# Adding four weighted corners of a sample: one strided VectorE reduction in place of two additions, in a deformable convolution on one Trainium2 core

## The reference

```
x = x + halo_attention(gn(x))     # 8x8 blocks, 14x14 windows, 4 heads
x = x + lstm(gn(x)) @ W_lin.T     # rows as sequences of 96 steps, hidden 128
x = x + deform_conv(gn(x))        # this is where the change lies
x = x + M @ blocks(gn(x)) @ M.T   # 8x8 blocks
```

```
x_off = g_lt * gather(qx_lt, qy_lt) + g_rb * gather(qx_rb, qy_rb)
      + g_lb * gather(qx_lt, qy_rb) + g_rt * gather(qx_rb, qy_lt)
x_off = x_off * mask              # (b, c, h, w, 9)
out   = conv3x3_stride3(x_off)
```

## Time and profile before

| | |
|---|---|
| median of three runs | 4143.36 us (4128.45 to 4147.88) |
| the profiled execution | 4145 us |
| its span | 4143.0 us, mean TensorE clock 0.67 |
| TensorE busy | 2422.6 us (58%) |
| VectorE busy | 2127.4 us (51%), 4233 instructions |
| ScalarE busy | 1085.4 us (26%) |
| GpSimd busy | 2652.4 us (64%), 2614 instructions |
| chain of work that ended last | GpSimd's gathers L563 47%, issue 14% |

### The profile page before, as it was taken

One profiled execution on the slowest core, in us unless ns is written; L12 is line 12 of the kernel. 1 busy time (PEld: TensorE's weight loads), 2 busy tenths in 40 slices (PEclk: granted clock), 3 DMA queues, 4 the chain that ended last, 5 costly groups with the idle time before them and its releaser, 6 DMA issues.

```text
span 4143.0 us, 53002 instructions
## 1 busy us (share of the span) xinstructions
PE 2422.6 (58%) x19232; PEld 1995.3 (48%) x19232; DVE 2127.4 (51%) x4233; ACT 1085.4 (26%) x2749; POOL 2652.4 (64%) x2614
## 2 busy tenths in 40 slices
PE   4877776787777658857776478657775211111112
PEld 3656664565666646636665356446664211111112
DVE  4753225787444568855445678644447323222222
ACT  2643332443322324423223144322221100000000
POOL 1000004777777767777777777777777777777775
PEclk9976667777566677866667678756667555555555
DMA  5531003663311246633113266431113212111111
GB/s 178 176 87 31 1 1 125 185 182 102 87 50 50 89 137 181 171 80 87 51 50 104 76 191 180 108 93 50 50 49 112 73 53 62 52 51 51 52 52 49
DMA packets 192844, 373.96 MB, mean 90 GB/s; under 512 B 59312, under 2 KB 89264, under 8 KB 192576
## 3 DMA queue, kind: packets, MB, share of 16 engines
q1 hardware_dynamic: 107256, 198.54, 15.8%
q0 software_dynamic: 82944, 170.04, 15.4%
q10 hardware_dynamic: 2384, 2.00, 0.2%
HBM read 265.15 MB, written 104.33 MB: 89 GB/s over the span
## 4 chain that ended last, share of the span: by engine, by line
POOL 47%; issue 14%; PE 1%; DVE 0%; ACT 0%; POOLq 0%; DMA 0%; DVEq 0%; ACTq 0%
POOL got L563 47%; PE bank L1290 0%; PE bank L1234 0%; PE gates L1500 0%; PE bank L1295 0%; PE gates L1491 0%; PE bank L1275 0%; POOLq L560 0%; ACT kp L627 0%; DVE k L899 0%; DVE k L905 0%; DVE got L844 0%; DMA got<-sample_table,index 0%; ACT q L608 0%; DVE red L846 0%
## 5 line engine op out<-in xcount | busy, mean ns | idle before, releaser
L563 POOL DMA_INDIRECT got<-sample_table,index x2592 | 2639.0, 1018 | 1435.1 <-issue 774.4
L1416 PE MATMUL gates<-hist,whh 128*128 128x96 f32 x3040 | 638.8, 379 | 303.5 <-DVE hist L1094 302.5
L1234 PE MATMUL bank<-turned,wout 128*128 128x96 f32 x1728 | 325.2, 369 | 748.3 <-DVE x L859 507.0
L1416 PEld LDWEIGHTS gates<-hist,whh 128*128 128x128 f32 x3040 | 576.6, 283 | 374.2 <-DVE hist L1094 372.8
L844 DVE TENSOR_TENSOR got<-got,weight 128x1152 f32<-128x1152 f32 x288 | 391.0, 1358 | 689.6 <-DMA got<-sample_table,index 689.1
L1234 PEld LDWEIGHTS bank<-turned,wout 128*128 128x128 f32 x1728 | 313.6, 281 | 764.4 <-DVE turned L853 758.7
L1087 DVE TENSOR_TENSOR prod<-sig,gc 128x192 f32<-128x192 f32 x384 | 133.9, 349 | 633.3 <-ACT sig L714 633.3
L925 DVE TENSOR_REDUCE mx<-gates 128x2 f32<-128x392 f32 x576 | 295.7, 553 | 137.2 <-PE gates L1313 127.3
L1406 PE MATMUL gates<-xs,wa 128*128 128x192 bf16 x768 | 256.0, 333 | 102.5 <-ACT sig L718 65.4
L646 ACT ACTIVATE pt<-gates 98x512 f32<-98x512 f32 x384 | 217.7, 593 | 287.7 <-PE gates L1327 283.3
L1408 PE MATMUL gates<-ones,bw 96*128 96x192 bf16 x768 | 261.8, 341 | 0.0
(11 more groups left out here) (134 smaller groups left out, 3505.9 us busy)
## 6 DMA issues: line engine op xcount, KB each, us to landing
kst<-k_parts SPq DMA_DIRECT2D x96, 441.0 KB
got<-sample_table,index POOLq DMA_INDIRECT x2592
qst<-q_parts SPq DMA_DIRECT2D x96, 288.0 KB
k_parts<-kp SPq DMA_DIRECT2D x24, 882.0 KB
k_parts<-kp SPq DMA_DIRECT2D x24, 588.0 KB
q_parts<-qp SPq DMA_DIRECT2D x24, 576.0 KB
sample_table<-tab SPq DMA_DIRECT2D x8, 1568.0 KB
q_parts<-qp SPq DMA_DIRECT2D x24, 384.0 KB
```

Of the source, the lines that this page charges most:

```text
L563: pool.indirect_dma_start(out=got[:, uu % RING, n, :], out_offset=None, in_=tables[p], in_offset=bass.IndirectOffsetOnAxis(ap=at, axis=0)) ...
L1234: mm = pe.matmul(out_ps[n % 2][:, at:at + GN], wout[:, tap, :], turned[:, k % 2, tap, :], start=(tap == 0), stop=(tap == NTAP - 1))
L1416: mm = pe.matmul(gate[n][:, h:h + W], whh[:, HID * g:HID * (g + 1)], hist[:, (t - 1) % HIST, :], start=False, stop=True, skip_group_check= ...
```

## The change

The tile `red` and the semaphore `summed` are gone. In `unit`, behind the multiplication, one `tensor_reduce` over the innermost axis reads `got` of the slot seen as (tap, channel, corner), so that the four corners of a channel, 32 numbers (128 bytes) apart, follow one another, and writes `samp` directly. It carries the signal `reduced`, on which GpSimd's ring slot and the transpose now both wait. The wait for `samp_turned` stands in front of it.

```diff
--- before.py
+++ after.py
@@ -210,7 +210,6 @@
         index = sb("index", [P, SLOTS2, CH, NTAP], I32)
         weight = sb("weight", [P, SLOTS2, CH, NTAP, 4])
         got = sb("got", [P, RING, NTAP, 4 * C])
-        red = sb("red", [P, NTAP, 2 * C])
         samp = sb("samp", [P, NTAP, C])
         turned = sb("turned", [P, 2, NTAP, GN])
 
@@ -380,7 +379,6 @@
         gathered = [sem(f"gathered{i}") for i in range(RING)]
         weighted = sem("weighted")
         reduced = sem("reduced")
-        summed = sem("summed")
         samp_turned = sem("samp_turned")
         convolved = sem("convolved")
         rows_added = sem("rows_added")
@@ -843,11 +841,9 @@
                 w = weight[:, chunk, uu % CH].rearrange("p n k -> p (n k)").unsqueeze(2).to_broadcast([P, NTAP * 4, C])
                 dve.tensor_tensor(corners, corners, w, ALU.mult).then_inc(weighted, 1)
                 dve.wait_ge(weighted, uu + 1)
-                dve.tensor_tensor(red[:, :, :], got[:, slot, :, 0:2 * C], got[:, slot, :, 2 * C:4 * C], ALU.add).then_inc(reduced, 1)
+                wait(dve, samp_turned, uu)
+                dve.tensor_reduce(samp[:, :, :], got[:, slot].rearrange("p n (k c) -> p n c k", c=C), AX.X, ALU.add).then_inc(reduced, 1)
                 dve.wait_ge(reduced, uu + 1)
-                wait(dve, samp_turned, uu)
-                dve.tensor_tensor(samp[:, :, :], red[:, :, 0:C], red[:, :, C:2 * C], ALU.add).then_inc(summed, 1)
-                dve.wait_ge(summed, uu + 1)
                 if i == 0:
                     wait(dve, convolved, k - 1)
                 dve.transpose(turned[:, k % 2, :, BLK * i:BLK * (i + 1)], samp[:, :, :]).then_inc(samp_turned, 1)
```

## The result

The change costs 2.95%: 4263.32 us in the median of six runs (4252.51 to 4278.82) against 4144.09 us of six runs of the kernel before (4128.45 to 4149.98), a ratio of 1.0295 with a 95% interval from 1.0269 to 1.0321. The forecast was 4262 us. The profiled execution took 4262.68 us, with a span of 4260.9 us.

What follows compares the result with a forecast made beforehand. VectorE's main stream was taken to bound until 1552 us, gathers from there to the end. 65.7 + 1.7 + 30.8 + 21.8 + 1.2 - 2.3 = +118.9 us on 4143.4 gave 4262 us, range 4136 to 4318.

Steps and rivals of the forecast that it cites:

- The reduction is slow because each number lies far from the last, not because of its kind: In each unit's reduction on VectorE: reads 128 bytes apart slow it from 1.36 us to 2.45 us; chance 0.66.
- free-stride rival: The reduction's stride costs nothing: 1.30 to 1.36 us, at most 0.1 us extra per unit, 4143 us; chance 0.24.
- Its size, 2.45 us: The strided reduction's duration, by L1050's factor of 1.9 on 1.04 ns per element; 1.19 us more per unit.
- lower bound of 4218 us: Low end of the forecast's own range: reduction 2.27 us, attention's share 0.71, 1.01 us extra per unit.
- LSTM of image 1, all 31 units in full: In image 1's LSTM each unit is the late side, so all 31 units count in full; 401 to about 438 us.
- Attention of image 1, 0.85 of each unit: In image 1's attention, 28 units count at 0.85, above the mean unhidden share of 0.71: 23.8 units.
- The first gather of image 2's round: At 1552 us: 65.7 us later from VectorE's main stream, plus 1.7 us for the slot's later release.
- Images 2 and 3: what the waits cover: Of 72.6 and 73.8 us added, data waits cover 41.8 and 52.0 us, leaving +30.8 and +21.8 us.
- The last stretch, nearly nothing: Behind 3222 us units lie under waits: +1.2 us for the last unit, -2.3 us for shorter gathers.
- The reduction does not hold GpSimd: Gathers starting during the one-input reduction are not held, as in L951: 0.94 us.
- Both rivals with a hold: Reduction holds GpSimd's gathers: fast, about 1.3 us, 4160 us, chance 0.04; or slow, 4475 us, chance 0.06.
- Signs: Expected profile: VectorE's gather waits 689 to about 600 us, GpSimd's slot waits 100 us or more, gathers' mean within 20 ns.

Runs made afterwards that it cites:

- dense kernel of part 1: The changed kernel with its reduction reading four neighbouring numbers (another sum): 4147.23 us, ratio 1.0002 to the kernel before; ratio 1.0015 on the 5355 us chip.
- VectorE's extra 0.79 us per unit: The kernel before plus one dense 576-number reduction per unit, result unread, behind the slot's release: 0.9975 on the 5355 us chip, 1.0199 (4233.63 us) on the 4154 us chip.

## Why the prediction was right

Its steps, one by one:

- *The reduction is slow because each number lies far from the last, not because of its kind.* Shown: dense 1353 ns, strided 2121 ns, and with the dense one the loss is gone (1.0002). The free-stride rival's own figure, 4143 us, is what the dense run gave (4147).
- *Its size, 2.45 us.* Too dear: 2.12 us. The factor of 1.9 came from L1050, which is of the fast kind with two reads at a time; a reduction loses 0.67 ns on 1.04 ns, a factor of 1.6. The other row, L1176 with 0.82 ns more per element, led to 2.27 us and was nearer (its own figures, 0.16 + 1152 x 1.86 ns, give 2.30 us, which moves the lower bound of 4218 us up by some 5 us). The text itself had named what spoke against L1050. Per unit that is 0.86 us in place of 1.19 us.
- *LSTM of image 1, all 31 units in full.* The mechanism is right: its steps with a unit went from 4.49 to 5.37 us, those without from 3.81 to 3.83 us. The stage grew by 28.9 us, 0.93 us per unit; to 431 us, not to 438, which is the size of the unit.
- *Attention of image 1, 0.85 of each unit.* Too kind. The stage grew by 26.0 us, and since the 4.3 us of data waits in it went to nothing, VectorE's own stream grew by 30.3 us: 1.08 us for each of 28 units, more than the 0.86 us that was put in. VectorE's waits for TensorE's scores grew in it from 30.0 to 38.4 us, and the granted TensorE clock fell from 0.73 to 0.70, so part of it may be matmuls that ran slower; that share was not measured by itself. The mean share of 0.71 was too low to begin with: image 0's window started at 20 us, but VectorE writes the first strip of its attention at 32.15 us, and that of image 1 at 696.48 us. From these to 290 and 1028 us it is 257.9 and 331.5 us, so 73.6 of 87 us were not hidden, 0.85.
- *The first gather of image 2's round.* Forecast 65.7 + 1.7 = 67.4 us later, measured 64.9 us. The dear unit and the kind share cancelled in the sum. The further 1.7 us for the slot cannot be told apart; moving the release alone behind the second addition cost nothing (1.0013).
- *Images 2 and 3: what the waits cover.* This is the step that was furthest off. It took the 41.8 and 52.0 us of waiting off in full. With the measured 0.86 us and 72 units that would leave 62 - 42 = 20 us for the second round and 10 us for the third; measured were 48.5 and 28.4 us. The waits for gathers did go to nothing, but other waits came. VectorE's waits for TensorE's scores in the attention of image 2, before and after (1504:1855 and 1564:1938 us), show it:

```profile
DVE mx L925 <- PE gates L1313: 27.8, 20, 4.0
```

```profile
DVE mx L921 <- PE gates L1309: 40.5, 21, 4.4
```

  In image 3's attention they went from 30.1 to 40.6 us. In the LSTM of the second round some 11 us more are in steps that hold no unit (their mean went from 3.68 to 3.86 us while the granted clock fell from 0.66 to 0.60), in that of the third 5 us (0.63 to 0.60). In the other runs on the chips of 4144 and 4154 us the clock of these LSTM stages lay between 0.58 and 0.68, so part of this loss may belong to the run and not to the change. Why the new waits came is argued, not tested: while VectorE waits for data, TensorE and ScalarE get ahead, and a wait that is filled takes that lead away too.
- *The last stretch, nearly nothing.* It gained 18.6 us where -1.1 us was forecast. GpSimd's group in this stretch, before and after (3234:4143 and 3370.6:4261 us), accounts for it:

```profile
L563 POOL DMA_INDIRECT got<-sample_table,index x689 | 668.1, 970 | 210.0 <-issue 210.0
```

```profile
L561 POOL DMA_INDIRECT got<-sample_table,index x680 | 652.7, 960 | 207.2 <-issue 207.2
```

  Busy and issue time are 878.1 us before and 859.9 us after, 18.2 us less. Nine gathers fewer are left, since GpSimd enters the stretch one unit further ahead (with 1912 gathers done in place of 1903, at 210 units on VectorE in both: 2.4 in place of 1.4 units): 9 x 1.27 = 11.5 us. The others are 10 ns shorter, 680 x 0.010 = 6.8 us: fewer holds, of which the forecast credited 2.3 us. The prediction left the longer lead out.
- *The reduction does not hold GpSimd.* Shown by 257 gathers at 0.94 or 0.95 us. Both rivals with a hold are out. (In the fast one the gather at 2602.48 us starts 0.3 us behind L849's start and not before its end; its price stays the same.) The Trainium skill (SBUF — State Buffer, Who interferes with whom), which the prediction left open, says so of `tensor_reduce` on trn2, and the trace agrees.
- *Signs.* VectorE's wait was to fall to about 600 us and fell to 507; GpSimd's slot waits were to be over 100 us and are 218.5; the gathers' mean was to stay within 20 ns and went from 1018 to 1003.

The sum, 118.9 us against 117.9 us by the spans, is closer than its terms deserve, and that is luck: a unit priced 0.33 us too dear and 17.5 us that the last stretch gave beyond the forecast were made up for by shares and covers that were too kind. Right were the cause, the side that is late in each stretch, and roughly where the loss falls.

## What to carry to other kernels

Fewer instructions are no gain where the one that stays reads one float of every 16 bytes: here 1.35 us became 2.12 us, more than the 1.22 us of the two dense additions that it replaced. If four summands must be innermost, let the producer (here, the table in DRAM) lay them side by side, or keep the dense additions. And when work is added to an engine that is not the bottleneck of the whole run, price it by stretch, and do not take waits off in full: of the 94 us in hand, about half was cover (2 x 62 us were added, 77 us were lost), though not a microsecond of these waits was left.

## What the runs showed of the hardware that was not expected

- **Two kinds of chip.** On two chips the kernel before takes 5355 and 5364 us. In the dense kernel of part 1, image 0's attention and LSTM, with no gathers beside them, take 288.6 and 343.1 us on the 5355 us chip and 290.3 and 342.5 us on the 4154 us chip; image 1's attention takes 586.6 us, against 343.3 us. TensorE's timelines of the dense kernel, first on the 5355 us chip, then on the 4154 us chip, in the same piece of attention (x16 in one line are sixteen matmuls one after another):

```profile
904.59 0.27 PE L1340 MATMUL bank<-pt,v 98*18 98x128 f32 x1 [0.33 <-issue]
905.30 0.39 PE L1340 MATMUL bank<-pt,v 98*18 98x128 f32 x2 [0.45 <-issue]
906.01 0.27 PE L1340 MATMUL bank<-pt,v 98*18 98x128 f32 x1 [0.32 <-issue]
907.41 0.63 PE L1340 MATMUL bank<-pt,v 98*18 98x128 f32 x3 [1.14 <-issue]
```

```profile
904.66 0.63 PE L1340 MATMUL bank<-pt,v 98*18 98x128 f32 x16
```

  On the first, matmuls that wait for nothing the profile shows come 0.7 us and more apart while gathers run. The cause was not tested. It seems that TensorE's stream sets the pace there; VectorE's extra 0.79 us per unit cost nothing (0.9975). A result of one chip need not hold on another of the same type.
- **A hold goes by where the operands lie.** In the kernel before, 303 gathers start in a multiplication with both inputs in SBUF; 241 of them take 0.96 us or more (up to 2.13 us), and each of these ends 0.81 to 0.83 us after the multiplication. With the weights in PSUM all of 224 take 0.94 or 0.95 us, at the same 1354 ns. Taking the hold away outside attention is worth 0.5% here.
- **The strided read costs in one step.** 1353, 1353, 2192 and 2121 ns at 4, 8, 16 and 128 bytes.
